# Causal attention rebuilt with keys on the partitions and kept scores, a part of its row sums on GpSimd

## The reference

```python
K, Q, V = (einsum('bpd,ihd->biph', layernorm(x), W) for W in (W_K, W_Q, W_V))
scores  = einsum('biph,biqh->biqp', K, Q)            # 16 heads, 2048 queries, 2048 keys
scores  = where(tril, scores, -1e10)
attn    = softmax(scores / 8, axis=-1)               # over the keys p
z       = einsum('biph,biqp->biqh', V, attn)
out     = einsum('bqf,df->bqd', z_flat, W_O);  x = x + out
```

## Time and profile before

| | |
|---|---|
| median of 3 runs (lowest, highest) | 1417.24 us (1416.24, 1417.28) |
| the profiled execution: its time, its span | 1418.09 us, 1416.4 us |
| busy in the span | PE 88%, DVE 68%, PE weight loads 60%, ACT 56%, POOL 10% |
| granted TensorE clock, mean | 0.943 of 2.4 GHz |

### The profile page before, as it was taken

How to read it: one execution, slowest core, us unless ns; L and a number is a source line. 1 busy time by engine, 2 the same in 40 slices (tenths; PEclk the granted TensorE clock), 3 DMA queues, 4 the chain that set the end, 5 groups by cost and what they waited for, 6 DMA issues and landing times. The chain is left out here.

```text
span 1416.4 us, 22644 instructions
## 1 busy us (share of the span) xinstructions
PE 1241.6 (88%) x7936; PEld 856.4 (60%) x7936; DVE 959.1 (68%) x2284; ACT 793.5 (56%) x2146; POOL 144.2 (10%) x174
## 2 busy tenths in 40 slices
PE   5999999999999999999999999999996294886285
PEld 3666666666667666666666576666664292443285
DVE  5776777677767767776777677667764263998254
ACT  5766566666657666666666666666652162232043
POOL 1000000000000000000000000000000553553433
PEclk9999999999999999999999999999996596997588
DMA  3950200020001002000200020020000121000023
GB/s 102 140 133 1 60 1 1 1 60 1 1 22 39 1 1 60 1 1 1 60 1 1 16 46 1 0 60 1 1 1 1 49 64 47 0 0 0 27 59 95
DMA packets 52677, 41.07 MB, mean 29 GB/s; under 512 B 14177, under 2 KB 41442, under 8 KB 52578
## 3 DMA queue, kind: packets, MB, share of 16 engines
q1 hardware_dynamic: 50018, 34.50, 11.6%
q0 software_dynamic: 2560, 5.26, 1.1%
HBM read 13.49 MB, written 9.48 MB: 16 GB/s over the span
## 5 line engine op out<-in xcount | busy, mean ns | idle before, releaser
L265 DVE TENSOR_REDUCE at_cmax<-at_ps 128x1 f32<-128x512 f32 (+3 forms) x576 | 350.0, 619 | 169.0 <-PE at_ps L441 167.5
L358 ACT ACTIVATE at_prob<-at_ps,at_nmax 128x512 f32<-128x512 f32 (+3 forms) x640 | 391.8, 622 | 56.4 <-DVE at_nmax L268 53.6
L451 PE MATMUL at_ps<-ident,at_prob 128*128 128x128 f32 x2176 | 307.2, 275 | 19.0 <-DVE at_probT L274 9.6
L451 PEld LDWEIGHTS at_ps<-ident,at_prob 128*128 128x128 f32 x2176 | 249.1, 140 | 91.5 <-issue 25.5
L468 PE MATMUL at_ps<-at_probT,at_v 128*64 128x256 f32 (+1 forms) x2304 | 295.0, 379 | 3.9 <-DVE at_probT L274 3.3
L365 ACT ACTIVATE at_probT<-at_ps 128x512 f32<-128x512 f32 (+1 forms) x288 | 165.3, 574 | 228.0 <-PE at_ps L451 226.5
L438 PE MATMUL at_ps<-at_k_st,at_q_parts 128*128 128x512 f32 (+3 forms) x640 | 283.4, 443 | 8.2 <-ACT at_prob L358 7.2
L441 PE MATMUL at_ps<-at_k_st,at_q_parts 128*128 128x512 f32 (+3 forms) x640 | 251.1, 394 | 0.0
L274 DVE COPY at_probT<-at_ps 128x512 f32<-128x512 f32 (+1 forms) x288 | 189.2, 657 | 69.3 <-PE at_ps L451 66.9
L468 PEld LDWEIGHTS at_ps<-at_probT,at_v 128*64 128x64 f32 x2304 | 141.7, 136 | 129.7 <-issue 51.4
L438 PEld LDWEIGHTS at_ps<-at_k_st,at_q_parts 128*128 128x128 f32 x640 | 120.8, 189 | 87.3 <-ACT at_prob L358 50.6
(11 more groups left out here) (184 smaller groups left out, 1254.0 us busy)
## 6 DMA issues: line engine op xcount, KB each, us to landing
at_q_parts<-at_q_parts SPq DMA_DIRECT2D x64, 256.0 KB, 4.3
f_xs<-slots_in SPq DMA_DIRECT2D x48, 64.5 KB, 1.9
slots_in<-zeros SPq DMA_DIRECT2D x2, 1536.0 KB, 19.0
wall<-in_L_ffn_w_dram SPq DMA_DIRECT2D x1, 2048.0 KB, 18.9
wall<-in_L_ffn_w_dram SPq DMA_DIRECT2D x4, 512.0 KB, 6.6
f_got<-slots_out SPq DMA_DIRECT2D x8, 256.0 KB, 3.6
out_dram<-x SPq DMA_DIRECT2D x4, 256.0 KB, 2.4
slots_out<-f_ys,f_back POOLq DMA_INDIRECT x48, 2.2
```

Source lines behind the costliest of these rows:

```text
L265: dve.tensor_reduce(cmax[:, u % SLOTS, c:c + 1], bank, AX.X, ALU.max).then_inc(s_cmax, 1)
L358: act.activation(prob[j % 2][u % 4][:, c * BANK:c * BANK + w], ring[k % RING][:, 0:w], ACT.Exp, bias=nmax[:, u % SLOTS:u % SLOTS + 1], acc ...
L451: last = pe.transpose(turn_ps[h][:, b * P:(b + 1) * P], prob[j % 2][2 * i + h][:, t * P:(t + 1) * P], ident[:, :])
```

## The change

The stage is rebuilt. The other stages are left as they are.

- **Keys lie on the partitions.** A unit (g, t) is one tile t of 128 keys against a chunk g of 512 queries, for both heads of a pair at once, so up to 128x1024 numbers in two PSUM banks. A pair has 4 chunks with 4, 8, 12 and 16 tiles; the last four tiles of each chunk are diagonal ones, with 512, 384, 256 and 128 queries. That is 40 units for a pair, worth 34 full ones.
- **Scores are kept.** ACT copies a unit's scores to a buffer `kept` in SBUF (16896 columns, used in turn), and they stay there until the maximum of the whole chunk is known. DVE keeps an elementwise maximum over the tiles (`max`). At a chunk's end PE turns it (`turn`), DVE reduces it to the negated maximum for each query (`peak`), PE spreads that over the partitions (`shift`) and ACT copies it to SBUF.
- **The maximum is then added by GpSimd** to each kept unit, in place (`sub`, L294). ACT takes the exponential in place (`exp`), and PE multiplies with V without any transpose (`value`).
- **Row sums** run along the partitions now. An elementwise sum over the tiles is built in `esum` (`sum`), by DVE, but for each fourth full tile (t % 4 == 3) by GpSimd (L290): one, two and three of them in the second, third and fourth chunk of a pair. PE adds the partitions up with a matrix of ones (`total`), DVE takes the reciprocal of 128x512 numbers (L354), and multiplies it into the result on its way out of PSUM (`leave`).
- The order of every engine comes from `attention_plan`, a list scheduler with a length for each step; it is worked out over all eight pairs at once.

The core of the diff; lengths of steps, semaphore waits on the ring of PSUM banks and the setup are cut.

```diff
+KEEP_COLS = 16896
+RING = 3
+def attention_plan(PAIRS, NC, TPC):
+    def adder(g, t):
+        return "pool" if t % 4 == 3 and t < tiles(g) - TPC else "dve"
...
+        step(("sub", g, t), "pool", 0.2 + 1.9 * part, ("act", "shift", g))
+        step(("exp", g, t), "act", 0.16 + 0.73 * part, ("pool", "sub", g, t))
...
+            # GpSimd
+                for kind, g, t in order["pool"]:
+                    rows = scores_of(g, t)
+                    if kind == "sum":
+                        pool.wait_ge(s_exp, unit(g, t) + 1)
+                        pool.wait_ge(s_sum, unit(g, t))
+                        pool.tensor_tensor(esum[:, :, :], esum[:, :, :], rows, ALU.add).then_inc(s_sum, 1)
+                        continue
+                    if t == 0:
+                        pool.wait_ge(s_shift, g + 1)
+                    pool.tensor_tensor(rows, rows, shift[g % 2][:, :, skip(g, t):BANK], ALU.add).then_inc(s_sub, 1)
...
             # VectorE
-                            dve.tensor_reduce(cmax[:, u % SLOTS, c:c + 1], bank, AX.X, ALU.max).then_inc(s_cmax, 1)
-                            dve.tensor_copy(probT[1][n % 2][:, 0:w], turn_ps[1][:, 0:w]).then_inc(s_probT[1], 1)
-                            dve.reciprocal(rinv[:, k, :], rsum[:, k, :]).then_inc(s_rinv, 1)
+                        # max
+                            dve.tensor_tensor(top[:, :, :], scores_of(g, 0), rows, ALU.max).then_inc(s_max, 1 + t)
+                        dve.wait_ge(s_max, unit(g, t))
+                        dve.tensor_tensor(some, some, rows, ALU.max).then_inc(s_max, 1)
+                        # peak
+                        dve.tensor_reduce(low[g % 2][:, :], ring[use_of["turn", g] % RING][:, :, :]
+                                          .rearrange("p h (i k) -> p (h i) k", k=P), AX.X, ALU.max, negate=True)
+                        # sum
+                                dve.tensor_tensor(esum[:, :, :], scores_of(g, 0), rows, ALU.add).then_inc(s_sum, 2)
+                                dve.tensor_copy(esum[:, :, :], rows).then_inc(s_sum, 1)
+                        dve.wait_ge(s_sum, unit(g, t))
+                        dve.tensor_tensor(some, some, rows, ALU.add).then_inc(s_sum, 1)
+                        # total, leave, add
+                        dve.reciprocal(rinv[:, :], o_ps[:, :]).then_inc(s_rinv, 1)
+                        dve.tensor_tensor(zT[g % 2][:, :], z_ps[:, :], rinv[:, :], ALU.mult).then_inc(s_zT, 1)
+                        dve.tensor_tensor(rows, o_ps[:, :].rearrange("p (t d) -> p t d", d=D), rows, ALU.add)
...
             # ScalarE
-                            act.activation(prob[j % 2][u % 4][:, c * BANK:c * BANK + w], ring[k % RING][:, 0:w], ACT.Exp,
-                                           bias=nmax[:, u % SLOTS:u % SLOTS + 1], accum_out=esum[...])
-                            act.activation(probT[0][n % 2][:, 0:w], turn_ps[0][:, 0:w], ACT.Copy)
+                        act.activation(scores_of(g, t), ring[use_of[("score", g, t)] % RING][:, :, 0:w], ACT.Copy)
+                        act.activation(shift[g % 2][:, :, :], ring[use_of["shift", g] % RING][:, :, :], ACT.Copy)
+                        act.activation(rows, rows, ACT.Exp).then_inc(s_exp, 1)
...
             # TensorE
-                                last = pe.transpose(turn_ps[h][:, b * P:(b + 1) * P],
-                                                    prob[j % 2][2 * i + h][:, t * P:(t + 1) * P], ident[:, :])
+                        for h in range(2):
+                            pe.matmul(bank, keys, q[:, 0, BANK - w:BANK], start=True, stop=False)
+                            if t >= TPC * (g % NC):
+                                pe.matmul(bank[:, 0:P], identr[:, :], maskr[:, :], start=False, stop=False)
+                            last = pe.matmul(bank, keys, q[:, 1, BANK - w:BANK], start=False, stop=True)
+                        # turn, shift
+                                last = pe.transpose(ring[...][:, h, cols], peak[g % 2][:, h, cols], ident[:, :])
+                                last = pe.matmul(ring[...][:, h, i * P:(i + 1) * P],
+                                                 low[g % 2][:, n:n + 1].to_broadcast([P, P]), ident[:, :])
+                        # value, total
+                            last = pe.matmul(z_ps[part, skip(g, t):BANK], v[:, t, part], rows[:, h, :],
+                                             start=t == 0, stop=t == tiles(g) - 1)
+                            last = pe.matmul(o_ps[DH * h:DH * (h + 1), :], ones[:, :], esum[:, h, :])
```

More of the change, by code:

```diff
@@ L71, in attention @@
[L71 to L138, removed]
@@ L140, in attention @@
-    order, last_order = ([it for it in issue_order(projections) if it] for projections in (True, False))
-    opening = [(step, i) for i in range(N_PJ) for step in ("project", "low")] + [("vproject", m) for m in range(N_V)]
+    CHUNKS = PAIRS * NC
+    order, adder, tiles, skip, width, first_unit, place, before = attention_plan(PAIRS, NC, TPC)
+    uses = [it for it in order["pe"] if it[0] in ("score", "turn", "shift", "project", "vproject")]
+    use_of = {it: n for n, it in enumerate(uses)}
@@ L143, in attention @@
+    reads = {"score": 0, "turn": 0, "shift": 0, "project": 0, "vproject": 0}
+    reader = []
+    for it in uses:
+        reads[it[0]] += 1
+        reader.append((it[0], reads[it[0]]))
     with ExitStack() as ctx:
@@ L220, in _ @@
-                second_copies(0)
-                fetch(sp)
-                for pair in range(PAIRS - 1):
-                    second_copies(pair + 1)
+                for n, (_, g) in enumerate(order["sp"]):
+                    sp.wait_ge(s_lo, g + 1)
+                    for h in range(2):
+                        here, there = slice(DH * h, DH * (h + 1)), slice(DH * (1 - h), DH * (2 - h))
+                        q = q_st[g % 2][h]
+                        sp.dma_start(q[there, :, :].bitcast(F32), q[here, :, :].bitcast(F32)).then_inc(s_second[g % 2], 16)
+                    if n == 1:
+                        fetch(sp)
@@ L497, in _, with free_bank @@
-                run(opening, 0, 0, True)
-                for pair in range(PAIRS - 1):
-                    run(order, pair, pair + 1, False)
-                run(last_order, PAIRS - 1, PAIRS, False)
+                pe.wait_ge(s_const, 4)
+                def free_bank(use):
+                    if use < RING:
+                        return
+                    kind, count = reader[use - RING]
+                    if kind == "score":
+                        pe.wait_ge(s_kept, count)
+                    elif kind == "turn":
+                        pe.wait_ge(s_low, count)
+                    elif kind == "shift":
+                        pe.wait_ge(s_shift, count)
+                    elif kind == "project":
+                        pe.wait_ge(s_lo, count)
+                    else:
+                        pe.wait_ge(s_v, count)
```

575 lines of the change are left out of this document (313 added, 262 removed).

## The result

The changed kernel took **1824.19 us** (median of four runs, 1823.33 to 1826.67), the kernel before 1417.26 beside it: a ratio of 1.2867 [1.2851, 1.2883], 407 us slower. The forecast was 1580, range 1310 to 1690. The sign is right; the size is off by 244 us, and the time lies outside the range.

A forecast was written before the change was run, and what follows sets the result against it. TensorE bounded attention before; afterwards DVE and GpSimd were to exclude each other at 150 us a pair. 21.6 + 1200 for eight pairs + 15 ends + 341 gave 1578 span, forecast 1580 us, range 1310 to 1690.

The forecast's parts named there:

- the deciding term: Attention stage: whether DVE and GpSimd can work side by side; if they exclude each other, 150 to 162 us a pair.
- Rival B: Attention stage: two-operand DVE reads go on beside GpSimd, 116 us a pair, 1320 us, faster; chance 0.20.
- D: Attention stage: only part of an instruction's length excludes the other engine, 122 to 132 us a pair, 1400 us; chance 0.06.
- the durations: Per pair: TensorE 110 us, ACT 88, DVE 69 two-operand plus 37 other; full max 1.22, reciprocal 4.0.
- Rival C: Attention stage: the clock falls below 0.73 and TensorE bounds again, 165 us a pair, 1700 us; chance 0.06.
- 150 = 69 + 81: Serial sum per pair: DVE's two-operand work, 69 us, plus GpSimd's at its low figure, 81 us.
- the other 38 of DVE lie beside GpSimd: Per pair: DVE's remaining 38 us, reciprocal included, run beside GpSimd's work.
- hidden fixed parts against these gaps: Per pair: fixed costs hidden under the other engine offset the buffer gap and GpSimd's sum waits, leaving 150 us.
- The ends: Start and end of the attention stage: filling, and exp to add behind the last sub, 15 us together.
- a sign: Before a chunk's first sub: GpSimd idle over 20 us a pair would mean the forecast fails upward.
- My 5 us: Before the fourth chunk's first sub: turn, peak, shift and its copy leave GpSimd without a sub, some 5 us.
- the move of the fourth sums costs 5 to 6 us a pair: Six sums a pair on GpSimd take 2.0 to 2.3 us each in place of 1.22 on DVE.

The follow-up runs named there:

- experiments 2: Changed kernel with max reading the scores in their PSUM bank instead of the kept SBUF copy: 1612.08 us, ratio 1.1366.
- experiment 3: Changed kernel with sub and all sums on DVE, GpSimd idle in the stage: 1656.80 us, ratio 1.1681.
- experiment 9: Changed kernel with GpSimd writing zeros (memset) where it added the shift, the maximum's subtraction left out: 1452.24 us, ratio 1.0243.
- Experiment 4: Changed kernel with a copy in place of the reciprocal, division left out: 1754.75 us, ratio 1.2372.
- experiment 1: Changed kernel with all row sums on DVE, none on GpSimd: 1833.65 us, ratio 1.2928.
- experiment 5: Changed kernel with the kept buffer cut from 16896 to 15360 columns: 1847.46 us, ratio 1.3027.
- experiment 7: Changed kernel with max reading PSUM, all sums on DVE, the running sum in PSUM and two pairs of ring banks for three: 1573.67 us, ratio 1.1094.
- after: The changed kernel itself, without any experiment's edit: 1824.19 us, ratio 1.2867 to the kernel before.
- 8: As experiment 7, with a reciprocal of 8 numbers for each partition, not 512, spread by TensorE and copied by ACT: 1558.31 us, ratio 1.1000.
- 11: As 8, with the planner told 2.35 us for a full sub, 2.10 before: 1502.41 us, ratio 1.0584.
- 10: Changed kernel with its planner told the measured lengths (sub 3.0, max 2.2, sum 2.0 and 2.6, reciprocal 3.35): 1895.35 us, ratio 1.3368.

## Why the prediction was right in its sign and wrong in its size

**Held: the deciding term.** That a two-operand `max` or `sum` and a GpSimd instruction exclude each other was inferred from L982's 1.20 against 0.341 us and the Trainium skill (SBUF — State Buffer, Who interferes with whom). 3.14 us for 1.21 in the trace and experiments 2, 3 and 9 show it. The Trainium skill's two conditions (two SBUF inputs; a GpSimd instruction that reads SBUF) agree with experiments 2 and 9, one each. Rival B (no exclusion) and D (a partial hold) fall: a round of 3.28 out of 3.47 is nearly whole. B's 1320 would have failed even without the hold, as experiment 9's 1452 says, where GpSimd's instructions are shorter besides: 116 us a pair was too little for this order and its dependences. Its steady pair takes 129.8, and an eighth of its stage 136.

**Held: the durations.** 1.22 for a full `max` (1.21 alone); 69 us of two-operand work on DVE for each pair (68.7 at lengths measured alone) and 37 of other work (35.3); ACT 88 (82.6); TensorE 110 at the full clock (126.4 at 0.84 in the row above, 106 by that clock). The reciprocal is 3.35 where I took 4.0: the 3.4 that I read from the two rows was the price, and the planner's 0.65 is wrong by five. Rival C's fall of the clock came only to 0.84, and TensorE, 126 of 177, isn't the bound.

**Mis-sized, with little effect: "150 = 69 + 81".** A full `sub` takes 2.36, not 2.00: near the second pair of rows (2.30), which I had used for the range's upper end and not for the 150. It makes 95.5 of the 81 (14.5 more). But about 11 of the serial sum of 164 overlap, as the fixed parts might; serial is 153.7 in a steady pair, 3.7 above the forecast's 150. That the two errors nearly cancel is luck.

**Failed: "the other 38 of DVE lie beside GpSimd", and "hidden fixed parts against these gaps".** The step took it that one of the two is always at work. In a steady pair neither is for 23.6 us. Of DVE's other work, 35.7 us with the copy (the forecast's 38), only 20.7 lie beside GpSimd. 3.7 + 23.6 makes the 27.3 by which 177.3 exceeds 150, and times eight that is 218. The ends were **mis-sized** too: 42.6 us where the sum has 15, 28 more. With 2 us less at the start and in the rest, these are the 244 missing.

What sets the steady 177.3 is shown in part. Experiment 4 shows one piece on the path: the reciprocal, put under GpSimd's work by the forecast, was worth 11.4 us a pair and 69 in the whole. Neither of GpSimd's two waits sets it alone: experiment 1 took the one before its own sums from 38.5 us to nothing and the one for the shift from 18.5 to 70.8, experiment 5 made them 25.1 and 31.8, and the steady pair stayed at 177.4 and 177.3. The prediction had named a sign (over 20 us a pair of idle time before a chunk's first `sub`, and it fails upward) and priced this gap as 5 us. It is 18.5 in a steady pair; only with the start of the stage counted in is it 236/8 = 29.5, so the sign was not clearly met, though the forecast did fail upward. My 5 us was the sum of the four steps from the last maximum to the shift; the gap of experiment 7 shows 9.0 for these four with the starts between them, and 14.3 ahead of them for the last scores and maxima in lists that hold other chunks' work. The rest of the 23.6 us, step by step, stays open.

**Wrong in its effect: "the move of the fourth sums costs 5 to 6 us a pair".** The serial part rose by 6.5 (experiment 1 against after), but the time did not follow: without these sums the pair is as long, and GpSimd's idle time stands before `sub` in place of its own sums.

**Where the 407 us lie.** A steady pair took 130.2 before (from one pair's first projection to the next pair's) and takes 177.3 now: 377 us over eight. The ends grew from 12 to 42.6 us, 30 more. With one operand of `max` in PSUM 212 us come back, the largest piece shown by a version that keeps all of the work. With all collisions of `max` and `sum` out but each chunk's first (7) 250 do; 8 and 11 bring 71 more. Of the last 84, some 42 lie in the steady pairs (135.5 for 130.2) and the others at the start and end of the stage. That the first of these are TensorE's own work and what is left of the waits for the shift (GpSimd is idle for 51.9 us of a steady pair in 11) is argued, not shown. Open stays which order would be best: no experiment gave the planner a model in which the two engines exclude each other; 10 only lengthened both. Nor was the start of the stage tried, where GpSimd is idle for 90.5 us before the first two chunks.

## What to carry to other kernels

Before work is moved to GpSimd, look where DVE's operands lie: if they are two in SBUF, and GpSimd reads SBUF, the two work nearly as one engine, and the slower one sets the price (2.36 for 1.22 us). Move an operand to PSUM first, and see the mean of the group come down to its length alone. And where an engine waits for a value that needs a whole chunk (a maximum, a sum), don't set its gaps against fixed costs: follow one end of a chunk through all queues, with the work of the other chunks that stands in them. Read a pair from the middle of the stage apart from the sums over all of it: the idle time at the start of the stage, divided by eight, looks like a loss of every pair.

## What the runs showed of the hardware

- The hold isn't fair. In most places DVE and GpSimd took turns (3.28 us a round), but one DVE addition stood for 17.38 us behind a row of GpSimd `sub` and another for 16.33. What decides between the two was not tested.
- A write-only GpSimd instruction (128x1024, 0.95 us) left two-operand DVE instructions at 1.22.
- A sum whose accumulator lies in PSUM costs DVE hardly more than one in SBUF: 1.229 (experiment 7) against 1.220 us (experiment 3) for 128x1024.
- DVE's reciprocal: 3.35 us for 512 numbers in each partition, 0.208 for 8, so 6.2 ns for each further number, about six times what a further number of an addition costs (1.0 ns, from the widths 1024 and 768 alone, 1.21 and 0.96).
- GpSimd's fp32 addition of 128x1024 takes 2.36 us alone, 2.33 from one start to the next.
